# Relative attention rebuilt: a block-diagonal query tile written by DMA, fp32 score rows in 32-row strips, a fused add and maximum, values in four column strips

## The chip, the cores and the metric

The kernel runs on one core of a Trainium2 chip. Its engines, each with its own queue of instructions, are PE (TensorE: matmuls and transposes into the eight PSUM banks), ACT (ScalarE), DVE (VectorE), POOL (GpSimd) and SP (SyncE, which issues the DMAs here). The metric is the device time of one execution in microseconds (us), lower is better. The kernel before takes 4999.79 us, the median of 3 runs that went from 4998.96 to 5003.04 us.

## The reference

The input is a batch of 8 sequences of 512 rows with 128 features. Eight layers follow one another, each `x = x + layer(layernorm(x))`: attention A, a mixture of 8 experts, attention B, the same experts, a linear attention, an adapter with two chosen experts, the relative attention and the adapter again. The change touches the relative attention alone:

```python
def srel_skew(x):                       # b, h, n, n
    v = jnp.pad(x, ((0, 0), (0, 0), (0, 0), (1, 0)))
    return v.reshape(b, h, n + 1, n)[:, :, :n, :]
qx = split_head(x @ Wq.T)               # 16 heads of 8 features
kx = split_head(x @ Wk.T)
vx = split_head(x @ Wv.T)
ns = jnp.arange(n) + (MAXLEN - n)       # n = 512, MAXLEN = 256
ex = rel_embed[ns].reshape(n, NH, HD).transpose(1, 0, 2)
srel = srel_skew(jnp.einsum('bhnd,hmd->bhnm', qx, ex))
qk = (jnp.einsum('bhnd,bhmd->bhnm', qx, kx) + srel) * inv_dim
mask = 1000000000.0 * jnp.triu(jnp.ones((n, n), dtype=x.dtype), 1)
atten = jax.nn.softmax(qk - mask, axis=-1)
out = jnp.einsum('bhnm,bhmd->bhnd', atten, vx).transpose(0, 2, 1, 3).reshape(b, n, d)
return out @ Wp.T + bp
```

Each of the 16 heads needs the lower triangle of a 512 x 512 score matrix: a product of queries and keys, plus a relative term in which each query row is shifted against the one before it.

## The kernel before, in words

One turn of a loop handles one sequence; there are 8 turns of about 621 us each. Within a turn the layers run one after another, since each needs the whole result of the one before: attention A 82 us, experts 76, attention B 81, experts 76, linear attention 105, adapter 17, relative attention 161, adapter 23 (in turn 3, the one that the rows are from). Every engine's order is written out by hand, and engines wait for one another on semaphores. The sequence stands as 4 tiles of 128 rows; a layer begins with a norm (`pool_norm`, L437, raises the variance to the power -1/2 on POOL) and with four transposes (L795) which ACT copies to `xnT` (L601).

The relative attention (`pe_rel`, `act_rel`, `pool_rel`, `rel`) has three parts.

**Head.** PE projects queries (L802), keys (L803) and values (L805). Queries and keys are split into three bf16 parts each: ACT rounds (L606, L608), DVE takes the rest (L1324), and so on. PE then multiplies the parts with 0/1 matrices (`spread_q`, `spread_k`, L820) so that 48 rows of a head hold six pairs of parts one below another. ACT (L617) and DVE (L1339) copy these stacks to SBUF. The first two places are made ahead of the relative products, the others between them.

**Relative products.** For every query position 0 to 127 within a tile PE makes 6 matmuls of 64 columns (4 tiles x 16 heads), which multiply the embeddings `relT`, shifted by that position, with that query's features masked to one head for each column (L1145, 768 in all). The masked queries `q_masked` are made 16 positions at a time by DVE and POOL (L459), and the 64 columns of a position stand one behind another. DVE (L1582, L1583) and ACT (L727, L728, L731) copy the results to `sc`, the shifted scores in columns form (keys on partitions), and POOL zeroes what lies above the diagonal (L483, 4 instructions for every 16 positions).

**Scores.** Head by head: PE makes the query-key product from the 48-row stacks in columns form (L1165) and adds the causal mask by a matmul (L1167); DVE adds the result to `sc` (L1597); PE transposes the 10 blocks of a head to rows (L1178); DVE takes the maximum (L1602); ACT takes the exponential (L745); PE transposes the 10 blocks back (L1199); ACT (L754) and DVE (L1609) copy them; PE multiplies by the values with 8 + 1 columns per head (L830). After 4 heads the result is copied, transposed (L838) and divided (`heads_out`, L1345, L1346). The output projection follows (`pe_out`).

Attention A and B already work in another form, which the change takes over in part: fp32 scores in strips of 32 rows, one head for each strip (L885), a fused instruction on DVE that adds the mask and finds the maximum (L1367), and values with 32 columns per head, four heads in the four column strips (L924).

SP issues the loads at the start, and in each turn the load of the next sequence and the store of the finished one.

## Time and profile before

| | kernel before |
|---|---|
| median of 3 runs | 4999.79 us (4998.96 to 5003.04) |
| the profiled execution's own time | 4999.74 us |
| its span | 4998.0 us |
| PE busy | 4497.6 us, 90% of the span |
| DVE, ACT, POOL busy | 48%, 35%, 17% |
| mean granted clock of TensorE | 0.90 of 2.4 GHz |
| relative attention in turn 3 | 1711.1 to 1872.4 us |
| its relative products | 1725.0 to 1755.8 us |
| its scores | 1755.8 to 1864.4 us |

The time of the profiled execution is 0.05 us from the median, so what is worked out from its rows can be set against the median. The granted clock is a share of full speed: 1.00 is 2.4 GHz and 0.50 is 1.2 GHz, and a stretch in between had both. Matmul records overlap, since matmuls are pipelined: the time of one row with x96 runs from the first's start to the last's end, and the mean of one is longer than the distance between two starts.

### The profile page before, as it was taken

The numbers are of one execution on the slowest core, as the hardware profiler recorded it, in microseconds if no ns is written. First come the engines' busy times: TensorE is split into PE (matmuls) and PEld (weight loads), VectorE is DVE, ScalarE is ACT, GpSimd is POOL, SyncE is SP. The second block draws the span as 40 slices with busy tenths as digits, with TensorE's granted clock in tenths as the row PEclk, the third lists the DMA queues.
The fourth block names the chain that finished last, engine by engine and source line by source line (L and its number), as shares of the span: only waits on it lengthen the run. The fifth ranks groups of instructions, "written<-read, shape, count | busy, mean of one in ns | idle before, by whom it ended". The sixth has DMA issues, their size and how long they took to land.

```text
span 4998.0 us, 76578 instructions
## 1 busy us (share of the span) xinstructions
PE 4497.6 (90%) x30219; PEld 2825.7 (57%) x30275; DVE 2393.4 (48%) x6906; ACT 1724.4 (35%) x3496; POOL 842.3 (17%) x1313
## 2 busy tenths in 40 slices
PE   7988989889898898988989889898898998988989
PEld 4556545565455654557545575455754557545575
DVE  3435544355443654435544355444554445544455
ACT  2333433234332343323433234333343333433334
POOL 2003110030110301113011140111401114011140
PEclk8999979999799998999989999899998998988989
DMA  2000000000000000000000000000000000000000
GB/s 67 1 1 1 1 6 1 1 1 1 6 1 1 1 1 6 1 1 1 1 6 1 1 2 1 6 1 1 2 1 6 1 1 2 1 3 1 1 1 3
DMA packets 19571, 17.25 MB, mean 3 GB/s; under 512 B 2462, under 2 KB 18799, under 8 KB 19183
## 3 DMA queue, kind: packets, MB, share of 16 engines
q1 hardware_dynamic: 19183, 11.99, 0.8%
q8 instruction: 254, 4.16, 0.3%
q14 instruction: 134, 1.10, 0.1%
HBM read 9.89 MB, written 2.10 MB: 2 GB/s over the span
## 4 chain that ended last, share of the span: by engine, by line
PE 79%; POOL 7%; DVE 6%; ACT 5%; issue 3%; DVEq 0%; ACTq 0%; POOLq 0%; SPq 0%
PE banks L982 7%; PE banks L986 7%; PE banks L885 7%; PE banks L972 7%; PE banks L913 6%; PE banks L830 6%; POOL work L483 4%; PE banks L924 3%; PE banks L870 3%; PE banks L1178 3%; PE banks L1165 2%; PE banks L1199 2%; PE banks L1072 2%; PE banks L1045 2%; PE banks L1021 2%
## 5 line engine op out<-in xcount | busy, mean ns | idle before, releaser
L1367 DVE CUSTOM_DVE_ANT_0 work<-banks,mask_row 128x512 f32<-128x512 f32 (+3 forms) x1024 | 452.3, 489 | 260.7 <-PE banks L885 254.5
L885 PE MATMUL banks<-work 32*128 32x128 f32 (+3 forms) x2048 | 534.0, 550 | 24.6 <-DVE work L1367 24.6
L437 POOL TENSOR_TENSOR rstd<-rstd,half 128x1 f32<-128x1 f32 x256 | 134.2, 550 | 2470.6 <-DVE moments L1295 1899.7
L913 PE MATMUL banks<-work 32*128 32x256 f32 (+3 forms) x2048 | 527.6, 522 | 11.0 <-ACT work L643 9.1
L643 ACT ACTIVATE work<-banks 128x384 f32<-128x384 f32 (+1 forms) x768 | 374.6, 529 | 461.0 <-PE banks L913 455.2
L659 ACT ACTIVATE work<-banks 128x512 f32<-128x512 f32 (+1 forms) x384 | 228.9, 596 | 698.6 <-PE banks L982 698.4
L1439 DVE TENSOR_TENSOR work<-work,banks 128x512 f32<-128x512 f32 (+1 forms) x384 | 263.6, 686 | 355.5 <-PE banks L986 355.2
L982 PE MATMUL banks<-xnT,wg 128*128 128x512 f32 (+1 forms) x768 | 423.6, 635 | 0.0
L986 PE MATMUL banks<-xnT,wu 128*128 128x512 f32 (+1 forms) x768 | 412.0, 619 | 0.0
L972 PEld LDWEIGHTS banks<-wd,work 128*128 128x128 f32 (+1 forms) x3072 | 360.6, 191 | 57.3 <-issue 57.3
L885 PEld LDWEIGHTS banks<-work 32*128 32x128 f32 x2048 | 292.3, 222 | 166.9 <-DVE work L1367 110.4
L972 PE MATMUL banks<-wd,work 128*128 128x128 f32 (+1 forms) x3072 | 361.0, 274 | 0.0
L1597 DVE TENSOR_TENSOR work<-work,banks 128x512 f32<-128x512 f32 (+1 forms) x384 | 229.3, 599 | 269.5 <-PE banks L1167 235.3
L446 POOL TENSOR_SCALAR_AFFINE_SELECT work<-work 128x256 f32<-128x256 f32 x512 | 204.4, 408 | 913.3 <-ACT work L643 910.5
L913 PEld LDWEIGHTS banks<-work 32*128 32x128 f32 x2048 | 288.0, 202 | 87.0 <-ACT work L643 46.7
L795 PE MATMUL banks<-ident,xn 128*128 128x128 f32 x256 | 107.6, 420 | 205.6 <-DVE xn L1301 200.7
L830 PE MATMUL banks<-work,values 128*9 128x512 f32 (+3 forms) x1024 | 290.7, 433 | 0.0
L754 ACT ACTIVATE work<-banks 128x512 f32<-128x512 f32 x256 | 139.0, 594 | 377.5 <-PE banks L1199 377.5
L986 PEld LDWEIGHTS banks<-xnT,wu 128*128 128x128 f32 (+1 forms) x768 | 146.6, 191 | 210.1 <-issue 210.1
L1424 DVE SCALAR_TENSOR_TENSOR x<-banks,work,x 128x128 f32<-128x128 f32 x512 | 144.2, 344 | 248.3 <-PE banks L972 248.3
L745 ACT ACTIVATE work<-banks,work 128x512 f32<-128x512 f32 (+3 forms) x512 | 229.5, 543 | 43.6 <-DVE work L1602 43.6
L1602 DVE TENSOR_REDUCE work<-banks 128x1 f32<-128x512 f32 (+3 forms) x512 | 216.4, 482 | 23.3 <-PE banks L1178 23.3
(255 smaller groups left out, 7252.4 us busy)
## 6 DMA issues: line engine op xcount, KB each, us to landing
x_next<-in_L_attn_a_x_dram SPq DMA_DIRECT2D x8, 256.0 KB, 2.8
out_dram<-x SPq DMA_DIRECT2D x8, 256.0 KB, 2.2
wg<-in_L_ffn_Wg_dram SPq DMA_DIRECT2D x1, 1376.0 KB
wu<-in_L_ffn_Wu_dram SPq DMA_DIRECT2D x1, 1376.0 KB
wd<-in_L_ffn_Wd_dram SPq DMA_DIRECT2D x2, 512.0 KB
wk_l<-in_L_attn_a_Wk_dram SPq DMA_DIRECT2D x1, 512.0 KB, 7.2
wv_l<-in_L_attn_a_Wv_dram SPq DMA_DIRECT2D x1, 512.0 KB, 6.7
wq_l<-in_L_attn_a_Wq_dram SPq DMA_DIRECT2D x1, 512.0 KB, 6.8
```

The source lines that it names most:

```text
L643: eng.activation(prob4[:, G % 2, hh, C_AT[j]:C_AT[j] + C_N[j]], bank(3 + c % 3)[:, 0:C_N[j]], ACT.Exp).then_inc(s_exp, 1)
L659: eng.activation(silu[0:w, i % 2, :], bank(i % 2)[0:w, :], ACT.Silu).then_inc(m_silu, 1)
L745: eng.activation(r_prob[:, h % 2, at[t]:at[t] + (t + 1) * P], bank(bk)[:, col:col + (t + 1) * P], ACT.Exp, bias=r_neg_max[:, h % 2, t:t + ...
L830: m = eng.matmul(bank(bk)[row:row + HD + 1, P * s:T], values[:, s, h, :], p_cols[:, h % 2, at:at + T - P * s], start=(s == 0), stop=(s == ...
L885: m = eng.matmul(bank(k % 3)[:, col:col + N], q4[own, G, P * t:P * t + P], k4[own, G, 0:N], start=True, stop=True)
L913: m = eng.matmul(bank(3 + c % 3)[:, col:col + N], k4[own, G, P * s:P * s + P], q4[own, G, P * s:T], start=True, stop=True)
L972: m = eng.matmul(bank(4 + e % 2)[:, P * t:P * t + P], hidden[0:w, e % 2, j, P * t:P * t + P], wd[0:w, e, j, :], start=(j == 0), stop=(j == ...
L982: eng.matmul(bank(i % 2)[0:w, :], wg[:, e, f0:f0 + w], xnT[:, :], start=True, stop=True).then_inc(m_g, 1)
L986: eng.matmul(bank(2 + i % 2)[0:w, :], wu[:, e, f0:f0 + w], xnT[:, :], start=True, stop=True).then_inc(m_u, 1)
L1367: m = eng.tensor_tensor_reduce(out=summed[:, k % 2, col:col + N], in0=bank(k % 3)[:, col:col + N], in1=mask_row[:, T - N:T], scale=1.0, sc ...
L1439: eng.tensor_tensor(hidden[0:w, e % 2, j, :], silu[0:w, i % 2, :], bank(2 + i % 2)[0:w, :], ALU.mult).then_inc(m_h, 1)
L1597: eng.tensor_tensor(v, v, bank(k % 2)[:, 0:JOB_N[j]], ALU.add).then_inc(r_sum, 1)
```

## The change

The split into six bf16 pairs goes, and with it `spread_q`, `spread_k`, the stacks, the masking of queries and the mask matmul. In its place:

- **Queries on a diagonal.** The queries keep two bf16 parts (`q_parts`). POOL zeroes `q_diag` (128 partitions x 16384 bf16) once in each turn, ahead of the relative attention, and SP issues 16 DMAs (one for each head: 8 partitions x 2 parts x 512) that copy a head's features to its own 512 columns. The relative products read `q_diag` directly. For one position the 64 columns that a matmul reads stand 1024 bytes apart from head to head and 256 bytes apart from tile to tile. All 768 products follow one another.
- **Query-key products** are made in fp32 and in rows form. The projections come in sets of four column strips (`project`, 8 sets of 4 matmuls), four sets before the relative products and four in the first bursts of the scores.
- **Scores** run in 48 jobs: for each group of 4 heads, four jobs of tile 3 (512 columns), four of tile 2 (384) and four of tiles 1 and 0 (256 + 128). Three jobs are a burst. The product lands in one of banks 0 to 2, ACT copies it to a ring of 12 rows (`r_rows`), PE transposes `sc` to banks 3 and 4, DVE adds both and finds the maximum in one instruction (`tensor_tensor_reduce`), ACT takes the exponential in place, and two bursts later PE transposes back to banks 5 and 6.
- **Values** of a group of 4 heads are multiplied in four column strips (16 matmuls in `weigh_group`) once the group's 12 jobs are copied.
- The copy of the relative products multiplies by a triangular table (`strict`), and POOL's selects now put in the mask instead of zeros.

```diff
@@ SP, in each turn
+                sp.wait_ge(r_zero, 1)
+                sp.wait_ge(r_lo, 1)
+                for h in range(H):
+                    own = slice(HD * h, HD * h + HD)
+                    sp.dma_start(q_diag[own, :, h, :], q_parts[own, :, 0:T]).then_inc(r_qd, 16)
                 sp.wait_ge(x_done, 16)
@@ POOL, in each turn
                 pool_norm(eng, 5)
+                eng.wait_ge(xnT_ok, 6)
+                eng.memset(q_diag[:, :, :, :], 0.0).then_inc(r_zero, 1)
                 pool_norm(eng, 6)
@@ ACT
+            eng.activation(q_parts[:, 0, 1:T + 1], bank(0), ACT.Copy, scale=scale).then_inc(r_hi, 1)
...
+            def qk_rows_in(a):
+                eng.wait_ge(r_a, a + 1)
+                if a >= NROWS:
+                    eng.wait_ge(r_pT, a - NROWS + 1)
+                N = C_N[a % ROWS4 // G4]
+                eng.activation(r_rows[:, a % NROWS, 0:N], bank(a % 3)[:, 0:N], ACT.Copy).then_inc(r_rows_in, 1)
...
+            for b in range(BURSTS + 2):
+                if b < BURSTS:
+                    for a in range(BURST * b, BURST * b + BURST):
+                        qk_rows_in(a)
+                if 1 <= b <= BURSTS:
+                    for a in range(BURST * (b - 1), BURST * b):
+                        exps(a)
+                if b < 4:
+                    columns_of(4 + b, 7)
+                if b >= 2:
+                    copies(b - 2)
+                if b >= 7 and b % 4 == 3:
+                    group_columns(eng, 2, b // 4 - 1, 7)
@@ PE
-            pe_project(eng, w)
-            eng.wait_ge(a_res, 2)
             eng.wait_ge(a_v, 3)
-            pe_spread(eng, 0)
-            pe_spread(eng, 1)
+            for i in range(4):
+                project(i, 4 + i)
+            eng.wait_ge(r_qd, 16 * H)
...
                         for n, (rp, qp) in enumerate([(0, 0), (0, 1), (1, 0)]):
-                            m = eng.matmul(bank(k % 4)[:, 64 * (q % 8):64 * (q % 8) + 64],
-                                           relT[:, rp, first:first + P], q_masked[c % 2][:, qp, q % IC, :],
+                            q_now = q_diag[:, qp, :, :].rearrange("p h (t i) -> p i t h", t=NT)[:, q]
+                            m = eng.matmul(out, relT[:, rp, first:first + P], q_now,
                                            start=(n == 0), stop=(n == 2))
...
+            def shifted_rows(a):
+                if a >= 2:
+                    eng.wait_ge(r_max, a - 1)
...
+            def columns(a):
+                tiles, hh = row_tiles(a)
+                eng.wait_ge(r_p, a + 1)
+                if a >= 2:
+                    wait_copied(eng, a - 2)
...
+            for b in range(BURSTS + 2):
+                jobs = range(BURST * b, BURST * b + BURST)
+                if b < BURSTS:
+                    for a in jobs:
+                        qk_rows(a)
+                if b == 0:
+                    eng.wait_ge(r_diag, 4 * (P // IC))
+                for a in jobs:
+                    if b < BURSTS:
+                        shifted_rows(a)
+                    if b >= 2:
+                        columns(a - 2 * BURST)
+                if b < 4:
+                    if b >= 1:
+                        eng.wait_ge(p_st, 4 * NG + 4 + b)
+                    project(4 + b, 7)
+                if b >= 6 and b % 4 == 2:
+                    if b == 6:
+                        eng.wait_ge(p_st, 6 * NG)
+                    weigh_group(b // 4 - 1, range(NT))
+                if b >= 7 and b % 4 == 3:
+                    group_rows(eng, 2, b // 4 - 1, 7)
@@ DVE
-                    eng.tensor_tensor(v, v, bank(k % 2)[:, 0:JOB_N[j]], ALU.add).then_inc(r_sum, 1)
...
+                        m = eng.tensor_tensor_reduce(out=rows, in0=rows, in1=bank(3 + a % 2)[:, cols], scale=-1.0,
+                                                     scalar=-MASKED, op0=ALU.add, op1=ALU.min,
+                                                     accum_out=r_neg_max[:, a % NROWS, n:n + 1])
...
+                for b in range(BURSTS + 2):
+                    for a in range(BURST * b, BURST * b + BURST):
+                        if b < BURSTS:
+                            row_max(a)
+                        if b >= 8 and a == BURST * b and b % 4 == 0:
+                            heads_out(2, b // 4 - 2, 7, r_rden)
+                    if b >= 2:
+                        for a in range(BURST * (b - 2), BURST * (b - 1)):
+                            if vector_copies(a):
+                                copy_columns(eng, eng.tensor_copy, a).then_inc(r_pTv, 1)
```

`vector_copies` gives DVE the jobs of tile 3 and of tiles 1 and 0 (a tile-3 job in two instructions), and ACT those of tile 2.

On PE, at the start of the relative attention and up to the third piece of relative products, the order before is this; a row is the kernel's line, the operation, the output and the inputs, and the moving operand's partitions (or the strip's) by its columns.

```order
L795 MATMUL banks<-ident,xn 128x128 x4
L802 MATMUL banks<-xnT,w_r 128x512
L803 MATMUL banks<-xnT,w_r 128x512
L805 MATMUL banks<-w_r,xnT 128x128 x4
L820 MATMUL banks<-work,spread_q 128x512 x6
L820 MATMUL banks<-work,spread_k 128x512 x6
L1145 MATMUL banks<-work,relT 128x64 x96
L820 MATMUL banks<-work,spread_q 128x512 x6
L1145 MATMUL banks<-work,relT 128x64 x96
```

At the same place the changed kernel has these rows (L1047 is `project`, L1072 the relative products).

```order
L755 MATMUL banks<-ident,xn 128x128 x4
L1051 MATMUL banks<-xnT,w_r 128x512
L1053 MATMUL banks<-w_r,xnT 128x128 x4
L1047 MATMUL banks<-xnT,spaced_q_r 32x512 x4
L1047 MATMUL banks<-xnT,padded_k_r 32x512 x4
L1047 MATMUL banks<-xnT,spaced_q_r 32x512 x4
L1047 MATMUL banks<-xnT,padded_k_r 32x512 x4
L1072 MATMUL banks<-work,relT 128x64 x768
L1087 MATMUL banks<-work 128x512 x3
L1100 MATMUL banks<-ident,work 128x128 x12
```

The spread matmuls are gone from before and between the products, and the products are one piece.

On PE, in the scores, one head of the kernel before stands like this.

```order
L1165 MATMUL banks<-work 128x512
L1167 MATMUL banks<-mask_kq,identb 128x128
L1165 MATMUL banks<-work 128x384
L1167 MATMUL banks<-mask_kq,identb 128x128
L1165 MATMUL banks<-work 128x128
L1167 MATMUL banks<-mask_kq,identb 128x128
L1178 MATMUL banks<-ident,work 128x128 x10
L1199 MATMUL banks<-ident,work 128x128 x8
L1165 MATMUL banks<-work 128x256
L1167 MATMUL banks<-mask_kq,identb 128x128
L1199 MATMUL banks<-ident,work 128x128 x2
L830 MATMUL banks<-work,values 9x512
```

Two bursts of the changed kernel in its scores are these (L1087 is `qk_rows`, L1100 `shifted_rows`, L1110 `columns`).

```order
L1087 MATMUL banks<-work 128x512 x3
L1100 MATMUL banks<-ident,work 128x128 x4
L1110 MATMUL banks<-ident,work 128x128 x3
L1100 MATMUL banks<-ident,work 128x128 x4
L1110 MATMUL banks<-ident,work 128x128 x3
L1100 MATMUL banks<-ident,work 128x128 x4
L1110 MATMUL banks<-ident,work 128x128 x3
L1087 MATMUL banks<-work 128x512
L1087 MATMUL banks<-work 128x384 x2
L1100 MATMUL banks<-ident,work 128x128 x4
L1110 MATMUL banks<-ident,work 128x128 x3
L1100 MATMUL banks<-ident,work 128x128 x3
```

Transposes to rows and back now alternate within a burst, and the values stand outside it.

On POOL, from the last instruction of the linear attention to the adapter that ends the turn, the changed kernel has these rows (L415 is the norm's power, L521 the zeroing of `q_diag`, L439 the selects).

```order
L464 TENSOR_TENSOR work<-work 128x4x128 x3
L415 TENSOR_TENSOR rstd<-rstd,half 128x1 x4
L521 MEMSET work 128x16384
L415 TENSOR_TENSOR rstd<-rstd,half 128x1 x4
L439 AFFINE_SELECT work<-work 128x16x16 x32
L415 TENSOR_TENSOR rstd<-rstd,half 128x1 x4
```

The zeroing stands between the norm of the first adapter and the norm of the relative attention, and the masking of queries between the selects is gone.

## Rows read from the trace of the kernel before

**Rows 1.** Windows of turn 3: products, then scores; columns in the first line.

```profile
core 0: us, PE busy (x) PEld busy (x) DVE busy (x) ACT busy (x) POOL busy (x), PEclk, DMA share, GB/s
...
1725.00:1755.80 30.80, 30.20 (x799) 26.01 (x803) 25.52 (x44) 19.59 (x57) 26.98 (x30) 1.00 0.02 4
1755.80:1864.50 108.70, 104.63 (x593) 59.33 (x593) 62.33 (x137) 48.97 (x104) 2.36 (x6) 0.95 0.00 1
```

**Rows 2.** Timeline of PE, head and first products: start us, us, engine line op.

```profile
1721.26 2.34 PE L820 MATMUL banks<-work,spread_q 128*128 128x512 bf16 x5 [3.01 <-issue]
...
1725.01 2.96 PE L1145 MATMUL banks<-work,relT 128*128 128x64 bf16 x96
...
1729.11 2.96 PE L1145 MATMUL banks<-work,relT 128*128 128x64 bf16 x96
1732.13 1.24 PE L820 MATMUL banks<-work,spread_k 128*128 128x512 bf16 x5
1733.21 2.96 PE L1145 MATMUL banks<-work,relT 128*128 128x64 bf16 x96
```

**Rows 3.** Timeline of ACT and DVE, the first two parts of the queries.

```profile
1715.72 0.60 ACT L606 ACTIVATE work<-banks 128x512 bf16<-128x512 f32 x1 [2.16 <-PE banks L802]
...
1716.35 0.69 DVE L1324 SCALAR_TENSOR_TENSOR work<-banks,work 128x512 f32<-128x512 f32 x1 [3.75 <-ACT work L606]
```

**Rows 4.** Timeline of SP, three of the loads at the start.

```profile
8.76 0.27 SPq L400 DMA_DIRECT2D up_b<-in_L_ffn_up_b_dram  x1
9.07 0.39 SPq L400 DMA_DIRECT2D down_b<-in_L_ffn_down_b_dram  x1
9.50 0.51 SPq L401 DMA_DIRECT2D x_next<-in_L_attn_a_x_dram  x1
```

**Rows 5.** The page's DMA issues: KB each, us to landing.

```profile
x_next<-in_L_attn_a_x_dram SPq DMA_DIRECT2D x8, 256.0 KB, 2.8
out_dram<-x SPq DMA_DIRECT2D x8, 256.0 KB, 2.2
```

**Rows 6.** Timeline of POOL, a bf16 memset at the start.

```profile
1.25 2.67 POOL L514 MEMSET spread_q<- 128x3072 bf16 x1
```

**Rows 7.** Timeline of ACT and POOL around the first adapter.

```profile
1695.95 0.38 ACT L601 ACTIVATE xnT<-banks 128x256 f32<-128x256 f32 x1 [0.65 <-PE banks L795]
...
1710.12 2.10 POOL L437 TENSOR_TENSOR rstd<-rstd,half 128x1 f32<-128x1 f32 x4 [14.98 <-DVE moments L1295]
```

**Rows 8.** Groups by form, scores: form and count, busy us, mean ns, idle before.

```profile
L1178 PE MATMUL banks<-ident,work 128*128 128x128 f32 x160 | 22.4, 292 | 0.0
...
L754 ACT ACTIVATE work<-banks 128x512 f32<-128x512 f32 x32 | 17.4, 595 | 47.2 <-PE banks L1199 47.2
...
L745 ACT ACTIVATE work<-banks,work 128x512 f32<-128x512 f32 x16 | 11.1, 692 | 5.2 <-DVE work L1602 5.2
...
L1609 DVE COPY work<-banks 128x256 f32<-128x256 f32 x16 | 6.7, 419 | 4.1 <-PE banks L1199 4.1
```

**Rows 9.** Groups by form, attention A: the fused add and maximum.

```profile
L1367 DVE CUSTOM_DVE_ANT_0 work<-banks,mask_row 128x512 f32<-128x512 f32 x8 | 5.3, 689 | 1.2 <-PE banks L885 1.1
```

**Rows 10.** Timeline of PE, attention A: three 512-column scores in strips.

```profile
1284.90 1.13 PE L885 MATMUL banks<-work 32*128 32x512 f32 x6
```

**Rows 11.** Timeline of PE, attention A: values and rows of a group.

```profile
1313.54 2.36 PE L924 MATMUL banks<-work,values 128*32 128x512 f32 x32
...
1319.64 0.66 PE L838 MATMUL banks<-ident,xnT 128*128 128x128 f32 x4
```

**Rows 12.** Windows with the clock, two stretches of the scores.

```profile
1758.20:1768.40 10.20, 9.26 (x38) 5.97 (x39) 7.72 (x14) 1.89 (x4) 0.00 (x0) 0.50 0.00 0
1768.40:1867.40 99.00, 96.30 (x562) 54.38 (x560) 54.54 (x123) 45.45 (x97) 0.00 (x0) 1.00 0.00 1
```

**Rows 13.** Windows with the clock, two stretches of attention A.

```profile
1290.50:1293.90 3.40, 2.75 (x19) 2.13 (x17) 3.08 (x15) 0.16 (x1) 0.00 (x0) 1.00 0.01 2
1293.90:1307.60 13.70, 13.70 (x63) 9.28 (x64) 9.12 (x42) 4.12 (x8) 1.23 (x3) 0.50 0.00 0
```

More of the change, by code:

```diff
@@ L1230, in pe_rel @@
+            weigh_group(NG - 1, range(NT))
             group_rows(eng, 2, NG - 1, 7)
-            pe_out(eng, 2, w[:, 3, :], bp_row)
+            pe_out(eng, 2, w[:, 2, :], bp_row)
         @block.tensor
@@ L1605, in column @@
[L1605 to L1623 removed]
+                    below = strict[:, q8].unsqueeze(1)
```

488 lines of the change are left out of this document (162 added, 326 removed).

## The prediction

> **What bounds the kernel now.** I read the windows by stage first. In the relative products [rows 1] PE is busy 30.2 of 30.8 us at full clock, in the scores 104.63 of 108.7 us, so PE is the bound of both and DVE (62.33 us in the scores) and ACT (48.97) are not. Then the timeline of PE [rows 2]: from the start of one piece of 96 products to the next but one with six spread matmuls between them, 1733.21 - 1729.11 = 4.10 us pass, and in the head PE stands idle for 3.01 us while the parts are made. Then the groups of the scores by form [rows 8], and the attention A rows, since the new scores are built like that layer's [rows 9 to 11]. Last the windows with the clock [rows 12, 13]: the granted clock has two levels here, 0.50 and 1.00.
>
> All durations come from the profiled execution, 4999.74 us, which is the median within 0.05 us. The change lies inside one turn and there are 8 turns, so I sum per turn and multiply by 8. The set-up at the start loses some instructions on POOL and DVE; PE waits there for the loads, and I count nothing.
>
> **1. The start of the products.** Before, they start at 1725.01 [rows 2]. Now they wait for 16 DMAs that wait for the second part of the queries. The first product of the layer ends where ACT's rounding starts, 1715.72, and DVE's remainder ends at 1716.35 + 0.69 = 1717.04 [rows 3]; both stand first on their engines in the new kernel too. SP then issues 16 small DMAs one behind another. An issue takes 0.27, 0.39 or 0.51 us with about 0.04 us behind it [rows 4]; I take the middle one, as the shape (8 partitions, 2 pieces each) lies between: 16 x 0.43 = 6.9 us, last issue over at 1723.9. Landing takes 2.2 to 2.8 us for the two DMAs that the page shows [rows 5], both far larger, so I take 2.2: products at 1726.1 to 1726.2, **+1.2 us**. Bounds: 16 x 0.31 + 2.2 gives 1724.2 (-0.8), 16 x 0.55 + 2.8 gives 1728.6 (+3.6). The zeroing that SP also waits for: 16384 elements at 2.67 us / 3072 [rows 6] is 14.2 us or less (starts of two such memsets lie closer than one lasts), from 1696.35, when `xnT` is ready, to 1710.1 to 1710.6. Behind SP's new waits stands only the store of the result, due much later; the next sequence's load is ahead of them. POOL's next work, the norm's power, begins at 1710.12 after 14.98 us of idleness [rows 7]. So it is hidden, with nothing to spare: 0, up to +0.5.
>
> **2. The clock at the start of the products.** PE's other work in the head (values, four sets of projections) ends near 1721, and then it waits some 5 us. After the 3.01 us of waiting before, the clock was at 0.50 until about 1724, so 2.7 us of the work behind the gap was slow; in attention A it stayed at 0.50 for 13.7 us [rows 13] with PE busy throughout. The products are dense, so I stay near the first and take 4.5 us. A product has 64 columns, 53.3 ns at 1.2 GHz against 29.8 (below); 4.5 x (1 - 29.8 / 53.3) = **+2.0 us**, bounds +1.2 and +6.
>
> **3. The products without the spread matmuls.** Six spreads take 1.24 us [rows 2], so 96 products take 4.10 - 1.24 = 2.86 us, 29.8 ns each, and 768 take 22.9 us instead of 30.8: **-7.9 us**. This assumes that the new way of reading the queries, 1024 bytes from column to column, costs PE nothing; no row of before shows PE reading bf16 so, and I come back to it. Behind PE, ACT is busy 19.59 us [rows 1], of which the stack copies go, and DVE loses the masking of the queries; neither becomes the bound of 22.9 us. POOL keeps its selects and loses its masks.
>
> **4. The scores.** PE's own work shrinks: the mask matmuls go, the products come three strips at a time (1.13 us for three of 512 columns [rows 10]), the values of a group take 2.36 us [rows 11]. By rows it is 16 x 1.13 + 2 x 22.4 (transposes both ways [rows 8]) + 4 x (2.36 + 0.66) + 2.4 for the four late projections = 77 us. But the banks are tight and PE has to wait inside a burst. The chain of a burst of three tile-3 jobs: products 1.13, ACT's copy of the first 0.60 (as L754 [rows 8]), DVE's add and maximum 0.69 [rows 9], which frees the bank for the third job's transposes 0.60, their maximum 0.61 at DVE's pace, DVE's copy of an earlier job in two pieces 0.75 (two of L1609's 0.42 [rows 8] less overlap), for which the transposes back of the third job wait, 0.44, and handovers of about 0.3: 5.1 us. The other bursts have shorter or split jobs, and I take 4.8 on average, 16 x 4.8 = 76.8. Outside it: values, group rows and the wait for ACT's copy between them, 2.4 + 1.4 + 0.5 = 4.3 three times, 12.9; the last columns, values and rows, 9; the wait for POOL's last selects, 2.4 as before (POOL's 2.36 us behind the products [rows 1]); one table load 1.3; a stretch at low clock as before, 10.2 us there [rows 12], some 3.5. Sum 106, against 108.6: **-2.6 us**. Bounds: PE's work alone, 77, or -31; and at half clock throughout, PE's 2.17 us in each chain doubled, 16 x 2.2 + 12 = +47. The handovers carry the estimate; a tenth of a microsecond per burst is 13 us of the whole time.
>
> A rule of the Trainium skill speaks against this stage: "TensorE: Matmul & The Clock Gate", Part 4, says that transposes do not count as activity for the clock. By it the stage, with 320 transposes and gaps between them, would run at half clock, and the +47 above would be its value. The trace disagrees: in 99.0 us with the same 320 transposes the clock was 1.00 [rows 12]. I leave the sum as it is.
>
> Sum: +1.2 + 2.0 - 7.9 - 2.6 = -7.3 us per turn, x 8 = -58: **4942 us**.
>
> **Rivals.**
> - *Strided reading halves the products' pace (slower).* At 2.4 GHz a bf16 operand gives one column each 0.42 ns; fp32 transposes take twice that for a column (22.4 us / 160 = 140 ns for 128 columns with gaps [rows 8]), so PE may get only one address each 0.83 ns and reach the bf16 pace by neighbours. The new read has no neighbours. Then a product takes 53.3 ns (64 columns), or 56 with the present overhead; with 55, 768 take 42.2 us, and the low clock of step 2 costs nothing more, since it makes the same pace: 42.2 - 22.9 - 2.0 = +17.3 per turn, x 8 = +138, **5080 us**. It decides from a pitch of 39 ns (7.3 / 768 above 29.8). For it: no row excludes it, and the arithmetic fits. Against it: ACT and DVE copy these very products from PSUM with a stride and pay nothing visible, but they read at a slower pace. The Trainium skill says the same ("SBUF — State Buffer", its note on cachelines): two hits in a 16-byte line are needed for full bandwidth. No run here has shown it yet.
> - *Low clock comes back in the scores.* PE will be busy 77 of 106 us. In attention A a stretch with PE busy 2.75 of 3.4 us was followed by 13.7 us at 0.50 [rows 13]. If a third of the bursts runs so, 5.3 x 2.2 + 2 = 13.6 us are added, x 8 = 109: **5051 us**. Against it: before, the stage held 1.00 for 99 us, but with PE hardly waiting.
> - *The chain is longer by 0.45 us a burst*, by waits for exponentials or copies that I count as hidden: 16 x 0.45 x 8 = 58, **5000 us**, no change.
> - *The waits hide, and PE's work bounds the scores*: 77 + 2.4 + 9 = 88 instead of 106, -18 x 8 = -144: **4798 us**. For it: ACT and DVE have room. Against it: the bank waits above.
>
> **How the numbers follow.** Forecast 0.40 (its own range 4895 to 4988: chain 4.5 to 5.0 a burst, start -0.8 to +3.6); strided reading 0.33; low clock 0.11; longer chain 0.09; hidden waits 0.07. The range goes from 4895, leaving out the last one, to 5115, which takes in strided reading with the start's upper bound. A change within 0.2% (10 us) can't be told from none. Faster: 0.39 + 0.07 + 0.01 = 0.47; same 0.11; slower 0.42.
>
> **What would show it.** The distance between two relative products in PE's timeline: 30 ns or above 50, and the stretch from first to last product, 25 or 42 us. The first product 15 us (1726.1 - 1711.1) behind the norm's first transposes, with PE idle some 5 us ahead and the clock at 0.50. POOL's zeroing over just as the norm's power begins. Scores of 106 us, bursts 4.8 us apart, DVE as the releaser of the second transposes. The forecast is wrong if the products' pitch is above 39 ns, if a burst takes over 5.3 us, or if the clock in the scores is below 0.9.

## The result and the profile after

The changed kernel takes 5590.35 us, the median of 4 runs (5589.61 to 5592.88), against 5000.23 us of the kernel before (4998.96 to 5003.04): a ratio of 1.1178, 95% interval 1.1161 to 1.1195. Forecast were 4942 us, with a range up to 5115.

These are lines of its page: the span, the engines' busy time, the relative products (now L1072) and the DMAs to the diagonal tile.

```profile
span 5591.1 us, 77725 instructions
...
PE 4748.6 (85%) x30387; PEld 3245.9 (58%) x30387; DVE 2264.1 (40%) x7285; ACT 1795.5 (32%) x3680; POOL 810.5 (14%) x1272
...
L1072 PE MATMUL banks<-work,relT 128*128 128x64 bf16 x6144 | 681.1, 288 | 72.2 <-DMA work<-work 72.2
...
work<-work SPq DMA_DIRECT2D x128, 16.0 KB
```

681.1 us in 8 turns are 85 us a turn for products that took 30.8. The windows of the same three stretches in one turn are head, products and scores; the last two answer to [rows 1].

```profile
core 0: us, PE busy (x) PEld busy (x) DVE busy (x) ACT busy (x) POOL busy (x), PEclk, DMA share, GB/s
1868.40:1887.50 19.10, 9.52 (x46) 4.07 (x46) 2.44 (x6) 3.94 (x7) 1.10 (x3) 0.68 0.08 14
1887.50:1972.50 85.00, 84.98 (x768) 84.88 (x768) 12.09 (x32) 14.03 (x45) 14.68 (x32) 0.50 0.00 1
1972.50:2086.20 113.70, 83.49 (x626) 54.50 (x624) 52.27 (x200) 63.61 (x140) 0.33 (x1) 0.89 0.00 1
```

PE is busy for all of the 85 us of products, with the clock at 0.50 throughout. The table sets the stages beside one another. A turn is cut at the start of the norm's first transpose, of the first product, of the last product and of the output projection behind the last group (us, medians over the turns):

| a turn | before | after | difference | forecast |
|---|---|---|---|---|
| head, up to the first product | 13.9 | 19.1 | +5.2 | +1.2 |
| products | 30.6 | 84.9 | +54.3 | -5.9 |
| scores | 108.9 | 113.9 | +5.0 | -2.6 |
| everything else | 467.9 | 478.5 | +10.6 | 0 |
| turn | 621.2 | 696.3 | +75.1 | -7.3 |

Eight times 75.1 are 601 us and the spans differ by 593; most of the difference lies at the start, since the first turn reaches the relative attention's norm only 3.7 us later than before (472.3 against 468.6 us), not 10.6. "Everything else" is in the main one place, the first adapter, 17.1 us before and 29.9 after; the output projection, the last adapter and attention A got 2.1 us shorter together. The adapter's timeline, where start and duration are the first two columns:

```profile
1840.78 0.69 DVE L1436 TENSOR_REDUCE work<-xnT 128x1 f32<-128x512 f32 x1 [0.84 <-ACT xnT L533]
...
1840.80 13.75 POOL L521 MEMSET work<- 128x16384 bf16 x1 [1.25 <-ACT xnT L533]
1841.50 13.13 DVE L1437 TENSOR_SCALAR work<-work 128x128 f32<-128x128 f32 x1
...
1854.69 0.60 PE L1027 MATMUL banks<-gateT,work 128*128 128x8 f32 x2 [12.12 <-DVE work L1437]
```

POOL's zeroing of the diagonal tile starts 0.02 us after DVE's L1436. The next DVE instruction, a multiplication of 128 x 128 elements that took 0.23 us before, ends with the memset, 13.13 us later, and PE waits behind it. The head, where SPq is SP's queue:

```profile
1873.63 0.69 DVE L1471 SCALAR_TENSOR_TENSOR work<-banks,work 128x512 bf16<-128x512 f32 x1 [3.73 <-ACT work L667]
1874.40 11.72 SPq L389 DMA_DIRECT2D work<-work  x16
...
1887.52 4.70 PE L1072 MATMUL banks<-work,relT 128*128 128x64 bf16 x41 [8.97 <-DMA work<-work]
```

The 16 issues take 11.72 us, 0.73 each, against the 0.43 that I had taken from [rows 4]; the products start 1.4 us after the last one. At the norm before the relative attention POOL is in time: its memset ends at 1854.55, and the norm's power begins at 1867.40, late only because the adapter is.

### The profile page after: what moved, and what is told of

Same layout as the page of the kernel before. It is cut to its first block, busy times and chain, and to the rows that moved or that the text cites. A ratio compares the mean times of both kernels' runs of the same rounds, so it can differ in the third digit from the quotient of the medians.

```text
span 5591.1 us, 77725 instructions
## 1 busy us (share of the span) xinstructions
PE 4748.6 (85%) x30387; PEld 3245.9 (58%) x30387; DVE 2264.1 (40%) x7285; ACT 1795.5 (32%) x3680; POOL 810.5 (14%) x1272
## 4 chain that ended last, share of the span: by engine, by line
PE 77%; DVE 9%; ACT 7%; issue 4%; SPq 2%; POOL 2%; DMA 0%; DVEq 0%; ACTq 0%
PE banks L1072 12%; PE banks L899 6%; PE banks L903 6%; PE banks L802 6%; PE banks L889 6%; PE banks L830 5%; PE banks L841 3%; PE banks L787 3%; PE banks L1110 2%; PE banks L1087 2%; PE banks L989 2%; DVE work L1437 2%; PE banks L962 2%; PE banks L1100 2%; DVE work L1494 2%
## 5 line engine op out<-in xcount | busy, mean ns | idle before, releaser
L1072 PE MATMUL banks<-work,relT 128*128 128x64 bf16 x6144 | 681.1, 288 | 72.2 <-DMA work<-work 72.2
L1072 PEld LDWEIGHTS banks<-work,relT 128*128 128x128 bf16 x6144 | 679.0, 124 | 79.4 <-DMA work<-work 79.4
L802 PE MATMUL banks<-work 32*128 32x128 f32 (+3 forms) x2048 | 535.6, 550 | 24.6 <-DVE work L1274 24.6
L415 POOL TENSOR_TENSOR rstd<-rstd,half 128x1 f32<-128x1 f32 x256 | 134.0, 548 | 2502.9 <-DVE moments L1222 1801.2
L1346 DVE TENSOR_TENSOR work<-work,banks 128x512 f32<-128x512 f32 (+1 forms) x384 | 263.5, 686 | 354.9 <-PE banks L903 354.6
L1494 DVE CUSTOM_DVE_ANT_0 work<-work,banks 128x128 f32<-128x128 f32 (+3 forms) x512 | 236.6, 486 | 376.5 <-ACT work L694 328.1
L1110 PE MATMUL banks<-ident,work 128*128 128x128 f32 x1280 | 228.6, 302 | 178.6 <-DVE work L656 137.1
L1481 DVE TENSOR_TENSOR work<-banks,strict 128x384 f32<-128x384 f32 x128 | 71.4, 558 | 667.0 <-PE banks L1072 667.0
L1110 PEld LDWEIGHTS banks<-ident,work 128*128 128x128 f32 x1280 | 164.4, 155 | 210.2 <-ACT work L702 191.9
```

Source lines behind the costliest of these rows:

```text
L802: m = eng.matmul(bank(k % 3)[:, col:col + N], q4[own, G, P * t:P * t + P], k4[own, G, 0:N], start=True, stop=True)
L1072: m = eng.matmul(out, relT[:, rp, first:first + P], q_now, start=(n == 0), stop=(n == 2))
L1110: m = eng.transpose(bank(5 + a % 2)[:, col:col + P], r_rows[:, a % NROWS, col:col + P], ident[:, :])
L1346: eng.tensor_tensor(hidden[0:w, e % 2, j, :], silu[0:w, i % 2, :], bank(2 + i % 2)[0:w, :], ALU.mult).then_inc(m_h, 1)
L1494: m = eng.tensor_tensor_reduce(out=rows, in0=rows, in1=bank(3 + a % 2)[:, cols], scale=-1.0, scalar=-MASKED, op0=ALU.add, op1=ALU.min, acc ...
```

## The experiments

The runs come from two chips. The kernel before took 4999.71 us (median of 6) on the first and 5009.76 us (median of 9) on the second; the second holds "Another form at the place that waited", "Masked queries, the new scores as written" and the two runs with the next burst's products ahead. Where it says one run, there is one execution; the masked version with four of them spreads over 44 us (4853.2 to 4897.6), so a difference of 20 us between single runs says little by itself.

### The products

**Neighbours instead of strides.**

```diff
-                            q_now = q_diag[:, qp, :, :].rearrange("p h (t i) -> p i t h", t=NT)[:, q]
+                            q_now = q_diag[:, qp, :, :].rearrange("p h t -> p (h t)")[:, 64 * q:64 * q + 64]\
+                                .rearrange("p (t h) -> p t h", t=NT)
```

> The 64 columns of a relative product are read from 64 neighbouring elements of the diagonal tile instead of elements 1024 and 256 bytes apart; the DMAs, the zeroing and all waits stay, and the products have other values. Theory S (a strided bf16 read costs PE two of its clocks a column, and the products run at 1.2 GHz because the array is fed at half pace): products 29.7 ns apart at full clock after a first stretch at 0.50 of some 5 us, 25 us in all instead of 84.9; 8 x 60 = 480 us less, about 5110 us. Rival C (the clock fell in the wait for the DMAs and stays down for another reason): 53 to 55 ns apart at 0.50 throughout, 42 us, about 5250 us. Rival W (the pace comes from the weights, or from the tile having been written by DMA): still 110 ns, 5590 us.

One run: 5162.14 us. The windows of its products, the first 5 us and the rest, show PE busy (count), then the other engines and the clock:

```profile
1783.90:1788.90 5.00, 4.96 (x97) 4.97 (x98) 1.51 (x4) 0.94 (x3) 0.00 (x0) 0.52 0.01 3
1788.90:1808.60 19.70, 19.70 (x677) 19.63 (x673) 10.28 (x28) 13.11 (x42) 13.13 (x28) 1.00 0.02 4
```

The products take 24.6 us, theory S's 25. The head is the changed kernel's, 19.12 us, with the same wait in it, and the clock recovers after 5 us; so neither the wait nor the DMAs hold it down, and with the same weights and a tile written by the same DMAs the pace is back: rivals C and W fall. The total is 52 us above the expected 5110. By the medians over the turns the scores took 1.5 us more than in the changed kernel (115.3), the output projection 2.0 (9.1) and attention A 2.4 (79.1, in one turn 84.8), all with more of the low clock; why it falls there in one kernel and not in another was not found.

**A ladder of strides, and one of runs.** The 128 positions in eight pieces, 96 products each. In the cuts `u` is the position within its piece and `run` the length of a run.

```diff
+                            kind = [1, 1, 2, 1, 4, 1, 8, 1][q // 16]
+                            q_now = flat[:, u:u + 64 * kind:kind]
```

> The 128 positions of the relative products in eight pieces of 16 (96 products each), which read their 64 columns with the strides 1, 1, 2, 1, 4, 1, 8, 1 in elements of 2 bytes; values are others than the reference's. Theory S with a line of 16 bytes and two hits needed: stride 2 (8 hits become 4) and stride 4 (2 hits) cost nothing, 29.7 ns, and stride 8 (one element in a line) costs twice, 53 to 56 ns. Rival N (PE needs its very neighbour, one address each 0.83 ns): strides 2, 4 and 8 all cost twice. Rival T (two clocks of whatever length): at full clock 55 ns, at half clock 110 ns for the pieces with a stride.

```diff
+                            kind = [1, 1, -8, -4, -2, 1, -1, -1][q // 16]
+                            q_now = flat.rearrange("p (a b) -> p a b", a=64 // run)[:, :, run * u:run * u + run]
```

> The relative products again in eight pieces of 16 positions, now reading runs: 64 neighbours, 64 neighbours, 8 runs of 8 elements (16 bytes), 16 runs of 4, 32 runs of 2, 64 neighbours, and twice 64 single elements 256 bytes apart; values are others than the reference's. The ladder before gave 29, 32, 60.5 and 116 ns for strides of 1, 2, 4 and 8 elements, the 116 at both levels of the clock. Theory L (each 16-byte line that is touched costs 1.81 ns, 116 / 64, whatever the clock): 8 lines hide under 29 ns, 16 lines give 29 to 31, 32 lines 58 to 60, single elements 110 to 116 ns at 1.00 as at 0.50. Rival P (two hits in a line are enough): runs of 2 at 29 ns. Rival J (the jump between runs costs by itself): runs of 4 above 40 ns.

Single runs: 5257.76 and 5286.33 us. Each window is one piece of 96 products (its count takes in those that reach over an edge). In the first, neighbours, strides of 2, 4 and 8 elements, and neighbours again behind them:

```profile
1812.84:1815.69 2.85, 2.85 (x102) 2.85 (x99) 1.26 (x4) 1.87 (x6) 1.89 (x4) 1.00 0.02 6
1815.69:1818.76 3.07, 3.07 (x103) 3.07 (x100) 1.57 (x6) 1.87 (x6) 1.88 (x4) 1.00 0.03 5
1821.61:1827.45 5.84, 5.84 (x103) 5.84 (x100) 1.75 (x6) 1.87 (x6) 2.23 (x5) 1.00 0.01 3
1830.32:1841.47 11.15, 11.15 (x103) 11.15 (x100) 1.75 (x6) 1.87 (x6) 3.56 (x8) 0.62 0.01 1
1841.47:1846.52 5.05, 5.05 (x97) 5.05 (x96) 1.51 (x4) 1.87 (x6) 0.30 (x2) 0.50 0.00 0
```

In the second, runs of 8, 4 and 2 elements, then single elements twice:

```profile
1817.39:1820.19 2.80, 2.80 (x102) 2.80 (x99) 1.50 (x6) 1.87 (x6) 1.88 (x4) 1.00 0.00 0
1820.19:1823.03 2.84, 2.84 (x102) 2.84 (x99) 1.52 (x6) 1.87 (x6) 1.88 (x4) 1.00 0.03 6
1823.03:1828.55 5.52, 5.52 (x103) 5.52 (x100) 1.76 (x6) 1.87 (x6) 2.16 (x5) 1.00 0.01 3
1831.42:1842.05 10.63, 10.63 (x103) 10.63 (x100) 1.75 (x6) 1.87 (x6) 3.42 (x8) 0.66 0.01 2
1842.05:1852.57 10.52, 10.52 (x97) 10.52 (x96) 1.51 (x4) 1.87 (x6) 1.76 (x5) 0.50 0.00 0
```

Divided by 96, the first ladder gives 29.7, 32.0, 60.8 and 116 ns and, at the low clock, 52.6; the second gives 29.2, 29.6, 57.5, 110.7 and 109.6 ns. A product that touches 64 lines of 16 bytes takes 110 to 116 ns, with 32 lines 57 to 61, with 16 lines 30 to 32, with 8 lines 29: 1.7 to 1.9 ns for each line, or the pace of neighbours (29 to 30 ns), roughly whichever is longer. The rungs give the length of a line too: a step of 8 bytes (stride 4) costs half of a step of 16 bytes (stride 8), and a step of 256 bytes costs no more than one of 16. The last two windows say the second thing: at a clock of 1.00 in a third of the first and at 0.50 in the second, single elements take the same 110 ns. (From start to start: 111 ns ahead of the clock's fall and 111 behind it; with the stride of 8, 116 and 116.) So in the changed kernel the low clock costs the products nothing. Strided products also keep it low. In both ladders it fell during the piece with one element in a line, after 20 us at 1.00. In the changed kernel it was at 0.50 already after the wait of 8.97 us, and where neighbours had it back after 5 us, here it stayed there to the end of the products. Theory S had the cause, the strided read, and the wrong reason for the size (its two clocks a column, at 1.2 GHz, come near the measured 110 ns by chance); rivals N, P, J and T fall, theory L stands. The Trainium skill's note on cachelines in "SBUF — State Buffer" has the 16-byte line right; that two hits are enough does not hold for PE's bf16 reads here, two cost 57 to 61 ns and four cost 30 to 32.

**The same queries with runs of 4.**

```diff
-                            q_now = q_diag[:, qp, :, :].rearrange("p h (t i) -> p i t h", t=NT)[:, q]
+                            q_now = q_diag[:, qp, :, NT * q:NT * q + NT]
...
-            eng.activation(q_parts[:, 0, 1:T + 1], bank(0), ACT.Copy, scale=scale).then_inc(r_hi, 1)
+            eng.activation(q_cols(0)[:, :, 1:P], q_raw[:, :, 0:P - 1], ACT.Copy, scale=scale).then_inc(r_hi, 1)
```

> The queries lie in the diagonal tile with the four tiles of one position next to one another, so that a product reads 16 runs of 4 elements (8 bytes); ACT and DVE write them so, in two instructions each instead of one, and DMAs, zeroing and scores stay. Theory L: 16 lines a product, 29 to 31 ns apart, products in 25 us instead of 84.9 and the head longer by some 0.7 us: near the run with neighbouring elements, 5162 us, so 5160 to 5175. Rival J: products in 35 us or more, over 5240 us.

One run: 5133.33 us, products 24.3 us. One layout, with the same DMAs, takes 60.6 us out of a turn; the head grew by 1.3 us to 20.5, twice the 0.7 expected. The whole was faster than expected by 27 us, since the scores took 110.7 us instead of 115.3.

This run also shows what the clock costs in the scores. Its scores are the changed kernel's, instruction by instruction, and took 108.3 us in one turn and 117.0 us in another:

```profile
3081.60:3189.90 108.30, 77.61 (x630) 52.25 (x626) 52.28 (x202) 63.53 (x140) 1.88 (x4) 0.95 0.00 1
2436.80:2553.80 117.00, 86.31 (x631) 56.68 (x626) 52.32 (x202) 63.53 (x140) 1.88 (x4) 0.87 0.00 1
```

Of these, 10.2 and 30.7 us are at a clock of 0.50; the other turns lie between (17.1 us at 0.50: 110.7 us; 27.3 us: 113.9 us). The changed kernel's 113.9 us have 25.8 us at 0.50, the 108.9 us of the kernel before have 10.2. So with as much low clock as before the new scores take about what the old ones took, and the 5.0 us that they cost more in the changed kernel are, by these turns, the low clock's; no run changed the clock alone.

### The zeroing

```diff
-                eng.memset(q_diag[:, :, :, :], 0.0).then_inc(r_zero, 1)
+                for h in range(H):
+                    m = eng.memset(q_diag[:, :, h, :], 0.0)
+                m.then_inc(r_zero, 1)
```

> POOL's zeroing of the diagonal tile in 16 instructions of 1024 elements instead of one of 16384; nothing else. Theory Z (the adapter's tensor_scalar on DVE, 0.23 us before and 13.13 us now, waits until POOL's memset that is under way is over, since both want the same port): it now waits for one piece, 0.9 us at most, and the few others of its kind likewise; the adapter falls from 29.9 us to 17 to 21, 8 x 9 to 8 x 13 = 72 to 100 us less, 5490 to 5520 us. Rival Q (DVE waits for POOL's whole work, by a semaphore or by bandwidth): no change, 5590 us.

One run: 5535.69 us. The adapter takes 18.1 us. In its timeline:

```profile
1820.65 14.76 POOL L522 MEMSET work<- 128x1024 bf16 x16 [1.24 <-ACT xnT L535]
1821.35 0.34 DVE L1439 TENSOR_SCALAR work<-work 128x128 f32<-128x128 f32 x1
...
1825.32 0.88 DVE L1462 TENSOR_SCALAR work<-work,pair_of 128x4 f32<-128x4 f32 x1
...
1826.49 1.78 DVE L1466 TENSOR_SCALAR work<-upT,work 128x128 f32<-128x128 f32 x4
```

The tensor_scalars shown now take 0.1 to 0.7 us longer, a part of a piece (0.95 us) and never more, and four of them take 1.78 us where they took 0.88: theory Z. The total fell by 55 us, less than 8 x 11.9 = 95. By the medians attention A (79.4 us), the scores (115.3) and the output projection (9.0) took 6 us a turn more, with more of the low clock.

**Another form at the place that waited.**

```diff
-                eng.tensor_scalar(pool_rep[:, :], pooled[:, 0:1].to_broadcast([P, P]), 1.0 / T, None,
-                                  ALU.mult).then_inc(d_pool, 1)
+                eng.tensor_reduce(pool_rep[:, :], pooled[:, 0:1].to_broadcast([P, P]).unsqueeze(2), AX.X,
+                                  ALU.add).then_inc(d_pool, 1)
```

> POOL's one large memset stays; the DVE instruction that waited 13.13 us for it, a tensor_scalar of the adapter from SBUF to SBUF, becomes a tensor_reduce over an axis of one element (which leaves out the factor 1/T of the pooled mean, so that the gate's values differ). The tensor_reduce right ahead of it ran in 0.69 us beside the memset. Theory F (the form decides: tensor_scalar from SBUF to SBUF wants the port that the memset holds, tensor_reduce does not): the new instruction takes under 1 us, and the wait moves to the next tensor_scalar, which then ends at the memset's end; what follows that one takes 10.3 us, so the adapter falls from 29.9 to about 27 us, 8 x 3 = 24 us less, 5565 us. Rival G (every instruction of DVE that starts during the memset waits): the same 13 us at the same place, 5590 us.

One run: 5631.55 us. The memset, the replaced instruction, a later one with two inputs in SBUF, and the next tensor_scalar:

```profile
1851.86 13.75 POOL L521 MEMSET work<- 128x16384 bf16 x1 [1.24 <-ACT xnT L533]
1852.56 0.29 DVE L1437 TENSOR_REDUCE work<-work 128x128 f32<-128x128 f32 x1
...
1854.19 0.22 DVE L1444 TENSOR_TENSOR work<-work 128x64 f32<-128x64 f32 x1
...
1856.27 9.37 DVE L1457 TENSOR_SCALAR work<-work 128x8 f32<-128x8 f32 x1
```

The new form takes 0.29 us beside the memset, and tensor_tensor with two inputs in SBUF its usual 0.22. The ten other instructions of DVE up to the next tensor_scalar take their usual times as well. The tensor_scalar takes 9.37 us, to the memset's end. The form decides, theory F; that what they share is a port, as the expectation has it, no run shows. The Trainium skill ("GPSIMD Engine Reference", 1. Specifications) names two kinds of DVE instruction that contend with POOL, those in a 2-port mode and those with two SBUF inputs; here the trace shows a wait for tensor_scalar alone, beside a memset, which reads nothing; a POOL instruction that reads was not tried. The time was a miss: 5565 expected. The adapter still took 30.6 us, because PE now waited 8.22 us behind its projections and made the last matmuls at half clock (8 of L1037 in 2.05 us instead of 1.16). The scores (115.6 us) and the output projection (8.8) together took 3.5 us a turn more than in the changed kernel.

### The scores

PE's waits in the changed kernel's scores (in us, times, longest):

```profile
engine line waited for: us in total, times, longest us
PE banks L1110 <- DVE work L656: 17.1, 12, 1.6
PE banks L1110 <- ACT work L709: 5.2, 3, 2.1
```

**Copies between the maxima.**

```diff
                         if b >= 8 and a == BURST * b and b % 4 == 0:
                             heads_out(2, b // 4 - 2, 7, r_rden)
-                    if b >= 2:
-                        for a in range(BURST * (b - 2), BURST * (b - 1)):
-                            if vector_copies(a):
-                                copy_columns(eng, eng.tensor_copy, a).then_inc(r_pTv, 1)
+                        if b >= 2 and vector_copies(a - 2 * BURST):
+                            copy_columns(eng, eng.tensor_copy, a - 2 * BURST).then_inc(r_pTv, 1)
```

> In the scores DVE's copies of the burst two before stand between the maxima of the burst instead of behind all three; nothing else. In the trace PE waits 12 times for 1.4 to 1.6 us for the last DVE copy of each burst, ahead of the third job's transposes back. Theory B (the order on DVE makes that wait): the wait shrinks to some 0.5 us, 12 to 16 us less a turn, 8 x 14 = 112 us, about 5480 us. Rival A (the same wait moves to ACT's copies of tile-2 jobs or to the maximum, which comes later by a copy): 0 to 4 us a turn, 5560 to 5590 us.

One run: 5521.07 us. The same two waits:

```profile
PE banks L1110 <- ACT work L709: 6.4, 4, 2.1
...
PE banks L1110 <- DVE work L656: 0.9, 5, 0.2
```

The wait for DVE went from 17.1 to 0.9 us, the scores from 113.9 to 99.1 us, with as much low clock as in the changed kernel (24.0 us at 0.50 against 25.8): theory B. Of 8 x 14.8 = 118 us the total shows 69. Most of the rest went behind the scores (by the medians the output projection took 9.6 us instead of 7.1, all of it at 0.50 instead of 3.0 us, and attention A 78.8 instead of 76.7).

### Mended versions

**Masked queries, the new scores as written.** The masking by DVE and POOL of the kernel before takes the place of zeroing, DMAs and strides.

```diff
-                            q_now = q_diag[:, qp, :, :].rearrange("p h (t i) -> p i t h", t=NT)[:, q]
+                            q_now = q_masked[c % 2][:, qp, q % IC, :].rearrange("p (t h) -> p t h", t=NT)
```

> The queries masked as in the kernel before and read from neighbours, and the changed kernel's scores exactly as they were written (copies behind the maxima). It says what the new scores are worth by themselves. From the parts: head 10.9, products 30.0, scores 110 to 113 (with neighbouring reads 110.7 and 115.3 were seen), the rest 472: 623 to 626 us a turn, 4990 to 5030 us, no change or slightly slower than the kernel before. The forecast's own value for this stage, 106 us, would give 619 us a turn and about 4970 us.

One run: 5011.0 us against 5009.76 of the kernel before on the same chip: head 10.9, products 30.0, scores 112.9 (111.7 to 118.1 in the single turns, with 17.1 to 34.1 us at the low clock). The 3.6 us a turn that the head and the products win, the scores lose. As written they are worth nothing: what they save in work on PE (80.8 us busy in a turn whose scores took 111.7, instead of 104.6 of 108.7) comes back as waits and as low clock.

**With copies between.** The same, with DVE's order of the run above.

> The changed kernel's scores and projections, but with the queries masked by DVE and POOL 16 positions at a time as in the kernel before, in two parts, read from neighbouring elements: no zeroing, no DMAs; and DVE's copies between the maxima. Taken together from the parts measured so far: head 11 to 12 us (no spread matmuls, no wait for DMAs, but the first masks stand behind DVE's remainder: 2.7 us), products 29 to 31 us (DVE has masks and copies, 26.7 us or more), scores 99 to 101, the adapter 17.1 again: 610 us a turn against 621.2, 8 x 11 = 90 us less than before, 4910 us. Rival M (DVE's masks now stand with multiplications and the copies of the products; DVE becomes the bound and the clock falls there): products 36 us or more, 4960 to 5000 us.

4867.95 us, ratio 0.9726 (0.9706 to 0.9746): head 10.9, products 30.0, scores 97.1. Better than expected by 42 us; the profiled execution took 4897.6 us, near the expectation, and the four lie between 4853.2 and 4897.6. Rival M fell.

**Runs of 4, pieces, copies between, two queues.**

```diff
-                for h in range(H):
+                for h in range(H // 2):
...
+            eng.wait_ge(r_zero, 1)
+            eng.wait_ge(r_lo, 1)
+            for h in range(H // 2, H):
+                own = slice(HD * h, HD * h + HD)
+                eng.dma_start(q_diag[own, :, h, :], q_parts[own, :, 0:T]).then_inc(r_qd, 16)
```

> The changed kernel with four things mended: runs of 4 elements, POOL's zeroing in 16 pieces, DVE's copies between the maxima, and the 16 DMAs issued half by SP and half by ACT. Theory: head 8 x 0.73 = 5.9 us of issue instead of 11.7, less the second instruction for each part: 19.1 - 5.9 + 0.7 = 14 us; products 25; scores 99; adapter 18: 468 + 1 + 14 + 25 + 99 = 607 to 612 us a turn, about 4885 us, faster than the kernel before by 2%. Rival A (ACT's own copies wait behind its issues and the scores or products get longer) 4930 us. Rival K (the clock at the low level in places where it was high takes back up to 5 us a turn, as in the runs so far): 4925 us.

4884.34 us, ratio 0.978 (0.9758 to 0.9803), the expected 4885 us. The head of its timeline:

```profile
1684.65 1.32 ACT L674 ACTIVATE work<-banks 128x508 bf16<-128x508 f32 x1 [2.16 <-PE banks L1065]
...
1686.03 1.33 DVE L1485 SCALAR_TENSOR_TENSOR work<-banks,work 128x508 bf16<-128x508 f32 x1 [4.41 <-ACT work L675]
...
1687.44 6.10 SPq L394 DMA_DIRECT2D work<-work  x8
1687.45 5.81 ACTq L690 DMA_DIRECT2D work<-work  x8
...
1695.16 2.05 PE L1086 MATMUL banks<-work,relT 128*128 128x64 bf16 x35 [5.76 <-DMA work<-work]
```

Eight issues on each queue at the same time take 6.10 and 5.81 us, so the pace of 0.73 to 0.76 us belongs to a queue, and the head fell from 20.5 us (runs of 4, one queue) to 15.1.

**The next burst's products ahead.**

```diff
-                if b < BURSTS:
+                if b == 0:
                     for a in jobs:
                         qk_rows(a)
...
                     if b >= 2:
                         columns(a - 2 * BURST)
+                    if a == BURST * b + 1 and b + 1 < BURSTS:
+                        for c in range(BURST * (b + 1), BURST * (b + 2)):
+                            qk_rows(c)
```

> As the run with masked queries and copies between the maxima, and in addition PE makes the three query-key products of the next burst ahead of the last job of a burst instead of behind it. In that run DVE waits 22.1 us a turn for ACT's copies of these products and ACT 20.6 us for the products themselves. Theory (the chain product, ACT's copy, maximum is the period of a burst): 1.1 to 1.7 us less in each of 16 bursts, scores 97.0 to 70 to 80 us, 8 x 20 = 160 us, about 4710 us. Rival (the maximum and the transposes for it bound the burst, or ACT, 63 us busy of 97, does): 2 to 6 us a turn, 4820 to 4855 us.

4800.3 us, ratio 0.9582 (0.9569 to 0.9596). Between theory and rival: the scores fell by 10.0 us, from 97.1 to 87.1, not by 17 to 27. Not all of this is the order: the stage has 3.4 us at the low clock in most turns, where it had 20.5 us. At the price that the turns of the run with runs of 4 give (some 0.3 us for each), that is 5 to 6 of the 10 us (an estimate). Its products and scores:

```profile
1665.90:1695.90 30.00, 24.71 (x767) 24.26 (x768) 25.57 (x41) 14.32 (x45) 26.76 (x30) 0.94 0.01 3
1695.90:1783.00 87.10, 76.16 (x632) 52.47 (x627) 50.21 (x202) 62.84 (x140) 2.59 (x6) 0.98 0.01 1
```

**The two together.** The diagonal tile of the run with two queues, and the next burst's products ahead.

> As the run with runs of 4 elements, zeroing in pieces, copies between the maxima and the DMAs issued by SP and ACT, with the next burst's products made ahead. Its scores should come down by as much as in the run with masked queries, 16 to 26 us a turn, and its head and products stay: 4884 - 160 = about 4720 us, within 20 us of the one with masked queries. Rival: 4840 to 4870 us.

4787.65 us, ratio 0.9556 (0.9539 to 0.9573), the fastest of all, and 12.7 us from the one above, though 68 us above the expected value, for the same reason. Its products and scores:

```profile
1669.60:1694.00 24.40, 24.40 (x768) 24.40 (x768) 11.85 (x32) 14.39 (x46) 13.16 (x28) 0.93 0.02 4
1694.00:1779.40 85.40, 74.68 (x630) 51.05 (x626) 49.93 (x202) 62.79 (x140) 1.88 (x4) 1.00 0.01 2
```

PE is busy 74.7 of 85.4 us, and the stage is where the prediction's rival of hidden waits put it, at PE's own work with start and end (88 us). So there were not the 20 us left that I had expected.

## Why the prediction was wrong

- **Step 3, the products (-7.9 forecast, -5.9 with step 2; measured +54.3).** This is the step that failed. It put PE's strided reading at nothing, though no row of before showed it. The measured pitch is 110.6 ns instead of 29.8, and the products took 84.9 us. With neighbours the two steps hold well: 24.6 us against the 24.9 of the sum. The strided rival named the mechanism, gave it 0.33, and priced it at 55 ns: it reasoned from fp32's pace, one address each 0.83 ns (its own row, 140 ns for 128 columns, is 1.09), while a line costs 1.7 to 1.9 ns. Its 5080 us should have been 4942 + 8 x (84.9 - 24.9) = 5422. The bound was the mistake: with no row, the upper end was a factor of two from an argument, not a bound. The condition, a pitch above 39 ns, and the stretch to look at were right.
- **Step 1, the zeroing (0 forecast, +12.9).** I asked only whether POOL was free and whether it would be ready for the norm, and it was: the memset took 13.75 us against at most 14.2. I did not ask who else works at that time. DVE's adapter does, and its tensor_scalar waits for the memset's end.
- **Step 1, the DMAs (+1.2 forecast, +5.2).** 16 issues took 11.72 us instead of 6.9. My upper bound of 0.55 us per issue came from the three loads shown, though the same trace had one of 0.72 us (`wu`, at 10.60) and one of 3.59 (`wd`, at 11.36); cheap rows chosen from a list give no upper bound. Landing was quicker, 1.4 us instead of 2.2.
- **Step 2, the clock (+2.0).** Right where the products read neighbours: there the first 5 us of products are at the low clock, 53 ns each, against 4.5 us assumed. In the changed kernel itself it played no part.
- **Step 4, the scores (-2.6 forecast, +5.0).** The chain was right, and in the trace DVE's copy is the releaser of the third job's transposes, as listed. Two sizes were off. One is the low clock: the sum took one stretch of 10.2 us as before, and there are 25.8 us in four, which is some 5 us by the turns of the run with runs of 4. The other is the chain: at full clock the four bursts of the third group take 5.76, 4.99, 7.38 and 6.61 us (their products start at 2024.26, 2030.02, 2035.01, 2042.39, and the next at 2049.00), and less 2.3 for values and 1.6 for group rows that is 5.2 on average instead of 4.8. The rival of a longer chain had 5.25, so it was right as to the burst; but a turn with 10.2 us of low clock takes 108.3 us in all against the sum's 106, so that the terms outside the bursts must have been too dear by some 4 us. That part of the sum was near by two errors that cancel; it was not measured term by term.
- **The low clock in the scores** (0.11) came, as 25.8 of 113.9 us and not as a third of the bursts, and the mean clock of the stage, 0.89, is one of the signs that the prediction named (below 0.9). The rule on transposes did not bite: the last version holds 1.00 over 85.4 us with 320 transposes in five of its eight turns, as the kernel before did over 99 us [rows 12], where it is 298 of the 320. But other matmuls stood between them in both, and no run has transposes alone.

## What to carry to other kernels

Before a bf16 operand of a matmul is read with a stride, count the 16-byte lines that it touches. Here, for 64 columns, 16 lines cost 30 to 32 ns and 32 lines twice that; the 64 lines of the changed kernel were 60 us a turn, and a change of layout to runs of 4 took them away. A long instruction on an idle POOL is not free: look at which instructions DVE has during it, cut it into pieces, or put it where DVE has none of them. Where three engines hand a burst around, look at what stands ahead of the instruction that releases a bank: moving DVE's copies took 15 us of 114, and making the next burst's products earlier took 10 of 97. And look at the clock of the same stage turn by turn before you explain a few microseconds by an order of instructions: the same scores took 108 to 117 us.

## What the runs showed of the hardware

- PE's bf16 reads of 64 columns that touch 32 or 64 lines of 16 bytes cost 1.7 to 1.9 ns for each line, against 29.7 ns for 64 neighbours at 2.4 GHz; with 64 lines the price is the same at either level of the clock.
- Dense products with one element in a line let the granted clock fall from 1.00 to 0.50 in both ladders, though PE counts as busy all the time (10.63 of 10.63 us); in the changed kernel it never rose over their 85 us. With two elements in a line it stayed at 1.00 for the 5.84 us of the piece.
- A DVE tensor_scalar from SBUF to SBUF waits for a POOL memset under way (13.13 and 9.37 us), while tensor_reduce (0.29 us) and tensor_tensor with two SBUF inputs (0.22 us) run beside it without a wait.
- Writing has a price of stride as well: 508 bf16 elements written 8 bytes apart took ACT 1.32 us, against 0.60 for 512 neighbours [rows 3]. DVE took 1.33 us against 0.69, but it also read one input 8 bytes apart.
- A DMA of 8 partitions with two pieces takes a queue 0.73 us to issue (16 in 11.72 us), and two queues issue side by side (8 in 6.10 and 8 in 5.81 us).
- In the scores a microsecond at 0.50 instead of 1.00 makes the stage about 0.3 to 0.4 us longer (108.3 us with 10.2 of them, 117.0 with 30.7).
